# The product of gates and expert biases as one split product between the experts, with a dozen units in other slots

## The reference

```
x = x + attention(layernorm(x))                         # 16 heads of 64, rotary q and k, softmax
x = x + cross_attention(layernorm(x), context, mask)    # 16 heads of 64, + bout
x = x + experts(layernorm(x))

def experts(h):
    probs = softmax(h @ Wg)                             # 8 experts
    top_vals, top_idx = top_k(probs, 2)
    gates = top_vals / sum(top_vals)                    # two gates per token
    expert_out = h @ We + be                            # be: one bias row per expert
    return sum(gates * expert_out[top_idx])
```

## Time and profile before

| | |
|---|---|
| runs | 3580.51 us median of 3 (3579.56 to 3580.77) |
| profiled execution | span 3581.8 us from the first to the last instruction; no other time is given for it |
| PE busy | 3501.3 us (98%), 28992 products |
| PEld busy | 2949.8 us (82%) |
| DVE / ACT / POOL busy | 2358.7 (66%) / 2220.8 (62%) / 2121.2 us (59%) |
| DMA | 47.44 MB, 4.0% of the 16 engines' time for the main queue |
| chain of waits | PE 89%, DVE 5%, ACT 2%, issue 2%, POOL 2% |

### The profile page before, as it was taken

How to read it: one execution, slowest core, us unless ns; L and a number is a source line. 1 busy time by engine, 2 the same in 40 slices (tenths; PEclk the granted TensorE clock), 3 DMA queues, 4 the chain that set the end, 5 groups by cost and what they waited for, 6 DMA issues and landing times.

```text
span 3581.8 us, 80997 instructions
## 1 busy us (share of the span) xinstructions
PE 3501.3 (98%) x28992; PEld 2949.8 (82%) x28992; DVE 2358.7 (66%) x7401; ACT 2220.8 (62%) x6442; POOL 2121.2 (59%) x1928
## 2 busy tenths in 40 slices
PE   6899999999999999999999999999999999999998
PEld 5788888888888888888888888888888888888886
DVE  6666667666666666676666666666766667666665
ACT  5666666666666666666666666666666666666663
POOL 5555676555665556765556755566655567555662
PEclk8999999999999999999999999999999999999999
DMA  3100000000000000000000000000000000000000
GB/s 98 37 10 13 10 10 10 10 13 12 7 10 12 9 12 10 9 10 10 12 12 7 10 12 10 12 10 9 10 10 12 12 7 12 11 10 12 13 6 8
DMA packets 46796, 47.44 MB, mean 13 GB/s; under 512 B 8256, under 2 KB 43328, under 8 KB 46400
## 3 DMA queue, kind: packets, MB, share of 16 engines
q1 hardware_dynamic: 45696, 41.99, 4.0%
q10 hardware_dynamic: 704, 0.27, 0.0%
HBM read 33.86 MB, written 8.39 MB: 12 GB/s over the span
## 4 chain that ended last, share of the span: by engine, by line
PE 89%; DVE 5%; ACT 2%; issue 2%; POOL 2%; DMA 0%; ACTq 0%; POOLq 0%; DVEq 0%
PE unit_ps L536 19%; PE pT_ps L648 14%; PE oT_ps L665 14%; PE score_ps L632 11%; PE unit_ps L524 10%; PE wo_ps L690 10%; PE unit_ps L546 8%; DVE x L1021 1%; ACT probs L798 1%; POOL probs L1150 1%; DVE probs L936 1%; PE unit_ps L555 1%; DVE bn L863 1%; DVE x_in L1029 1%; ACT v_sb L744 1%
## 5 line engine op out<-in xcount | busy, mean ns | idle before, releaser
L1150 POOL TENSOR_TENSOR probs<-probs,inv_sum 128x512 f32<-128x512 f32 x1024 | 1062.1, 1041 | 956.4 <-DVE inv_sum L919 956.3
L787 ACT ACTIVATE pT<-pT_ps 128x512 f32<-128x512 f32 x1024 | 606.2, 594 | 136.1 <-PE pT_ps L648 135.5
L798 ACT ACTIVATE probs<-probs,neg_max 128x256 f32<-128x256 f32 x1024 | 508.9, 500 | 276.4 <-DVE probs L936 276.4
L648 PE MATMUL pT_ps<-ident,probs 128*128 128x128 f32 x4096 | 634.0, 279 | 13.2 <-POOL probs L1150 12.5
L648 PEld LDWEIGHTS pT_ps<-ident,probs 128*128 128x128 f32 x4096 | 451.8, 141 | 221.8 <-issue 204.0
L798 ACT ACTIVATE probs<-score_ps,neg_max 128x256 f32<-128x256 f32 x1024 | 476.6, 476 | 179.1 <-DVE neg_max L925 179.1
L665 PE MATMUL oT_ps<-pT,v_sb 128*64 128x256 f32 x4096 | 556.0, 392 | 4.4 <-ACT pT L787 4.0
L936 DVE TENSOR_SCALAR_CACHE_REDUCE probs<-score_ps,mask_add 128x256 f32<-128x256 f32 x1024 | 433.4, 480 | 104.8 <-PE score_ps L632 101.9
L536 PE MATMUL unit_ps<-xs_hi,w_lo 128*128 128x256 f32 x1536 | 460.1, 300 | 9.3 <-DVE swap L972 7.8
L536 PE MATMUL unit_ps<-xs_hi,w_hi 128*128 128x256 f32 x1536 | 436.6, 284 | 0.0
L536 PE MATMUL unit_ps<-xs_lo,w_hi 128*128 128x256 f32 x1536 | 436.1, 284 | 0.0
(11 more groups left out here) (121 smaller groups left out, 8573.0 us busy)
## 6 DMA issues: line engine op xcount, KB each, us to landing
x_in<-dram_x SPq DMA_DIRECT2D x32, 256.0 KB, 2.7
xn<-dram_ctx SPq DMA_DIRECT2D x32, 256.0 KB, 2.7
layer_out<-x SPq DMA_DIRECT2D x32, 256.0 KB, 2.2
swap<-dram_bout SPq DMA_DIRECT2D x32, 128.0 KB, 3.1
rope<-dram_be SPq DMA_DIRECT2D x32, 64.0 KB, 2.9
rope<-dram_we SPq DMA_DIRECT2D x5, 256.0 KB, 2.8
probs<-dram_sk SPq DMA_DIRECT2D x4, 256.0 KB, 5.1
x<-dram_cq SPq DMA_DIRECT2D x4, 256.0 KB, 3.2
```

Source lines behind the costliest of these rows:

```text
L648: last = nc.tensor.transpose(pT_ps[s % 2][:, k * T + t * P:k * T + (t + 1) * P], probs[:, hs % P_BUFS, t, k * P:(k + 1) * P], ident[:])
L787: nc.scalar.activation(flat(pT[:, s % 2, :, :]), pT_ps[s % 2][:], ACT.Copy).then_inc(pT_ready.sem, 1)
L798: last = nc.scalar.activation(dst, src, ACT.Exp, bias=neg_max[:, h % STATS, t:t + 1], scale=1.0 if h < H else -1.0, accum_out=row_sum[:, h ...
L1150: nc.gpsimd.tensor_tensor(weights, weights, inv.unsqueeze(2).to_broadcast([P, NT, T]), ALU.mult).then_inc(probs_ready.sem, 1)
```

## The change

Gates and biases are each taken as a high part (fp32r) and a low remainder, and the three products high x high, low x high and high x low are stacked along the 128 rows, so that one fp32r product gives the sum. Once, in the first pass, ACT and DVE split the biases and SP writes the parts to a DRAM tensor `be_parts` (rows of high, high, low and zeros, 32 each). In each pass SP loads them into the second half of `xs_hi` (slot 12), DVE copies the gates three times into 128 columns (slot 13, `gate_cols`), TensorE transposes those, DVE casts them to fp32r and subtracts for the low rows, in the first half of `xs_hi`. GT stands in slot 15 and BI in slot 16, between EX3 and EX4; the bias is added between those two experts' adds.

The table moves other units: V2 from slot 8 to 10, V3 from 10 to 13, EX3 from 14 to 15, K4 from 17 to 18, EX6 from 18 to 19, K5 from 19 to 22, Q5 from 21 to 20, V5 from 23 to 21, K6 from 22 to 26, Q6 from 24 to 23, K7 from 30 to 28, V6 from 27 to 29, V7 from 35 to 33. Some go from NOW to LATE or back, EX1 among them (now NOW). In slot 18 the order is EX5, the last self-attention projection, V4, K4, L2. The gate weights move to slot 7, the first layer norm (statistics and norm) one slot later. In slot 15 the projection now follows the units, in slot 27 it precedes them.

```diff
-    8: [("V", 2, 0, LATE), ("EX", 0, -1, LATE)],
-    9: [("EX", 1, -1, LATE)],
+    8: [("EX", 0, -1, LATE)],
+    9: [("EX", 1, -1, NOW)],
...
-    "gate weights": 8,
+    "gate weights": 7,
     "gate table": 8,
...
-        be_sb = rope[0:HD, 0, 0, 0:D]
-        gatesT, bout_sb = swap[0:HD, 0, 0:T], swap[:, 1, 0:D]
+        be_sb = rope[0:32, 0, 0, 0:D]
+        be_hi, be_lo = xf_hi[0:32, 0, 0:D], xf_lo[0:32, 0, 0:D]
+        gate_cols = xn[:, :, 0:P]
+        gatesT, be_rows = xs_hi[:, 0, 0:T], xs_hi[:, 1, 0:D]
...
+                    if s == AT["expert biases"] and exists(b, -1):
...
+                        sp.dma_start(be_rows.bitcast(F32), be_parts).then_inc(be_loaded.sem, 16)
...
-                        last = nc.tensor.transpose(ps[0:E, t * P:(t + 1) * P], gates[:, t, :], ident[:])
+                        last = nc.tensor.transpose(ps[:, t * P:(t + 1) * P], gate_cols[:, t, :], ident[:])
...
                         last = nc.tensor.matmul(ps[:, t * D:(t + 1) * D], gatesT[:, t * P:(t + 1) * P],
-                                                be_sb, start=True, stop=True)
+                                                be_rows, start=True, stop=True)
...
-                    nc.vector.tensor_copy(gatesT[0:E, :], ps[0:E, 0:T]).then_inc(gatesT_ready.sem, 1)
+                    nc.vector.tensor_copy(gatesT, ps[:, 0:T]).then_inc(gatesT_hi.sem, 1)
+                    dve.wait_ge(gatesT_hi.sem, gatesT_hi.at(b, off, 1))
+                    nc.vector.tensor_tensor(gatesT[32:64], ps[32:64, 0:T], gatesT[32:64].bitcast(F32),
+                                            ALU.subtract).then_inc(gatesT_ready.sem, 1)
...
+                        blocks = gate_cols.rearrange("p t (i e) -> p t i e", e=32)[:, :, 0:3, 0:E]
+                        nc.vector.tensor_copy(blocks, gates[:].unsqueeze(2).to_broadcast([P, NT, 3, E])) \
+                            .then_inc(gate_columns.sem, 1)
```

More of the change, by code:

```diff
@@ L98 @@
     1: [],
-    2: [("V", 0, 0, NOW), ("K", 2, 0, LATE)],
+    2: [("K", 2, 0, LATE), ("V", 0, 0, NOW)],
     3: [],
@@ L154 @@
     "norm 3": 5,
-    "gate weights": 8,
+    "gate weights": 7,
     "gate table": 8,
     "context": 11,
-    "mask": 13,
+    "mask": 14,
+    "gate columns": 13,
+    "expert biases": 12,
+    "expert biases split": 23,
     "statistics 2": [18, 0],
-    "norm 2": [18, 3],
+    "norm 2": [18, 1],
     "x to x1": 22,
-    "statistics 1": 24,
-    "norm 1": 25,
+    "statistics 1": 25,
+    "norm 1": 26,
     "last values": [17, 0],
@@ L166, with before_bias @@
     "residual 3": 3,
-    "projection first": [7, 15, 31],
+    "projection first": [7, 27, 31],
 }
-def bias_first(s):
-    return s % 2 == 0 and UNITS[s] and UNITS[s][0][0] == "BI"
+def before_bias():
+    added = sorted((s + late, 1 - late, n, kind) for s in UNITS for n, (kind, g, off, late) in enumerate(UNITS[s])
+                   if kind in ("EX", "BI"))
+    return [kind for _, _, _, kind in added].index("BI")
+BEFORE_BIAS = before_bias()
 def splits(b, s):
@@ L709, in body @@
                     for n, (kind, g, off, _) in enumerate(UNITS[s]):
-                        if exists(b, off) and not (n == 0 and bias_first(s)):
+                        if exists(b, off):
                             unit(b, s, n, kind, g, off)
@@ L836, in body @@
                         split_piece(j)
+                    if s == AT["expert biases split"] and isinstance(b, int) and b == 0:
+                        act.wait_ge(be_in, 16)
+                        nc.scalar.activation(be_hi, be_sb, ACT.Copy).then_inc(be_split, 1)
                 if isinstance(b, int) and b == -1:
@@ L1089, in body @@
                         gate_table(b, -1)
+                    if s == AT["gate columns"] and exists(b, -1):
+                        if exists(b, 0):
+                            dve.wait_ge(ctx_ready.sem, ctx_ready.at(b, 0, 1))
+                        else:
+                            dve.wait_ge(xf_turned.sem, xf_turned.at(b, -1, 1))
+                        dve.wait_ge(gate_step.sem, gate_step.at(b, -1, GATE_STEPS))
+                        blocks = gate_cols.rearrange("p t (i e) -> p t i e", e=32)[:, :, 0:3, 0:E]
+                        nc.vector.tensor_copy(blocks, gates[:].unsqueeze(2).to_broadcast([P, NT, 3, E])) \
+                            .then_inc(gate_columns.sem, 1)
+                    if s == AT["expert biases split"] and isinstance(b, int) and b == 0:
+                        dve.wait_ge(be_split, 1)
+                        nc.vector.tensor_tensor(be_lo, be_sb, be_hi.bitcast(F32), ALU.subtract).then_inc(be_split, 1)
                     if s == AT["mask"] and exists(b, 0):
```

90 lines of the change are left out of this document (58 added, 32 removed).

## The result

The changed kernel takes **3651.4 us** (median of 4 runs, 3650.0 to 3652.3), the kernel before 3580.4: ratio 1.020, 95% interval 1.019 to 1.021. Slower by 71 us: one round takes 111.57 us in place of 109.32, and 31 times 2.25 are 70. The prediction said 3602, range 3564 to 3614: the direction was right, the size a third of what came, and the time outside the range.

What follows compares the result with a forecast made beforehand. TensorE, busy 98% of the span, bounds the kernel. Per round -0.67 - 1.65 + 0.95 + 1.71 + 0.39 = +0.73 us, over 31 rounds +22.6, drain -0.8, added to 3580.5: 3602 us, range 3564 to 3614.

Steps and rivals of the forecast that it cites:

- New gap 2: Slots 8 to 11: gate weights ahead of DVE's reciprocal delay head 8; +1.71 us per round, bounds 0.5 to 1.9.
- shared-port rule: Gate table on DVE: a two-SBUF-input step or cast waits out a whole POOL instruction; steps of 1.1 us expected.
- Rival B: Slots 8 to 11: a table step gets between POOL's rope steps; gap about 1.0 us, 3580 us total; chance 0.13.
- New gap 1: Slot 18: L2 waits for the norm with only V4 and K4 between; +0.95 us per round, bounds 0.8 to 1.1.
- Q4's wait: Behind the late L2: Q4 waits 0.24 us for xs_lo, one of the small new gaps.
- The product: Product of gates and biases: two fp32r products over 128 rows, 0.24 us; -0.67 per round, bounds -0.5 to -0.8.
- L3 put at nothing: Slot 6: the prediction has no term for a new wait of L3.
- all of the 1.65 as gone: Whole round: all old gaps in TensorE's starts, 1.65 us per round, go; new ones are priced separately.
- POOL's stretch without a break: Slot 30 to slot 1: POOL has rope and probabilities throughout; head 0's probabilities end 0.46 us before its transposes.
- rival C: From slot 30 to slot 1 POOL becomes the bound; 1 us more per round, 3634 us; chance 0.07.
- I count 1.0 back: Slot 30 to slot 1: 1.44 us of TensorE products leave; 1.0 regained as K7's split no longer delays DVE and ACT.
- T0: Transposes of head 0's probabilities: a small new wait of 0.05 us per round.

Runs made afterwards that it cites:

- runs 1 to 3: Changed kernel with gate weights back in slot 8: 3630.6 us; changed kernel with V2, V3 back in slots 8, 10: 3605.8; kernel before with gate weights in slot 7: 3582.3.
- run 6: Changed kernel with V0 before K2 in slot 2, as before the change: 3631.8 us.
- run 9: Changed kernel with the product of gates and biases read as fp32, same 128 stacked rows and same place: 3675.1 us.
- Run 11: Kernel before with the split product alone, in its old slot 20: 3585.8 us, ratio 1.0013.
- run 5: Changed kernel with V6 in slot 30 instead of 29: 3663.6 us.
- 15: Changed kernel with V2, V3 back in slots 8, 10, V0 before K2, V6 in slot 30, Q0 LATE, V7 in slot 35: 3582.7 us.
- run 4: Changed kernel with Q0 before K7 in slot 28 instead of behind it: 3686.0 us.
- runs of 14: Changed kernel with V2, V3 back in slots 8, 10, V0 before K2, V6 in slot 30, Q0 LATE in slot 28: 3594.6 us.
- runs 7: Changed kernel with K5 in slot 18 before L2, and Q6, Q7, K6 moved forward to slots 22, 23, 25: 3821.1 us.
- run 10: Kernel before's table with the split product, gates turned in slot 15, product in slot 16, slot 20 without a unit: 3675.8 us.
- run 12: Kernel before with the split product in slot 20, V5 moved to slot 21 and Q6 to slot 23: 3726.4 us.

## Why the prediction was right in direction and wrong in size

**New gap 2: right.** 1.71 forecast, 1.71 measured (slot 12's scores at 13.24, forecast 13.25), by the mechanism named: the steps beside POOL of 1.29 and 1.25, and runs 1 to 3 show its two halves, order and cover. The shared-port rule of the Trainium skill ("SBUF — State Buffer", "Who interferes with whom") is borne out for a case that the trace of before did not show: a cast of 16 elements waits for a whole POOL step, 1.29 us for 0.17. Rival B, a race in which a table step gets ahead of POOL, did not happen in the changed kernel: the cast lost it in all 31 rounds. But it is real. In the 13 traces in which the cast meets that rope step it starts 0.016 to 0.029 us behind it in all 403 rounds, and runs through in 61 of them, 27 of these in run 6. In 8 of the 10 runs that have both kinds of round, the rounds in which it runs through are shorter by 0.24 to 0.28 us.

**New gap 1: right, too small.** 0.95 forecast, 1.11 measured, 0.15 behind L2 that I hadn't counted, and 0.15 of Q4's wait (0.24 forecast). The chain was right to the norm's end; left out were the 0.14 from there to L2's start, and that K4's low part, queued behind the norm, would hold up EX6. Bounds of 0.8 to 1.1 didn't hold what stands behind L2.

**The product: right, its saving set too high.** 0.67 forecast, 0.53 by rows; 0.64 is what run 9 gives for the same stacked product in fp32, in its new place. I had set 0.24 for a group that costs 0.32 behind transposes. Run 11 adds what I didn't ask: in its old place the saving is worth nothing, since slot 22 waits it away.

**L3 put at nothing was the step that failed.** The prediction takes "all of the 1.65 as gone" and prices new gaps one by one; for L3 in slot 6 there is no term, and it waits 0.81. The forecast followed POOL's stretch without a break to head 0's transposes and stopped there, but the stretch runs on to norm 3, and L3 waits for that. Runs 5, 6 and 15 take the 0.81 apart: 0.42 go with V0 ahead of K2 (V0's copy then leaves ACT early enough for the split of Q2, for which POOL waits), an order that the prediction doesn't mention; 0.36 go with V7 back in slot 35 (with V6 already in slot 30; V7 alone was not run). With V7 in slot 33 TensorE has 1.44 us less to do between slot 34 and slot 6, POOL as much as ever. V6 alone leaves L3's wait as it is (run 5).

The step inside rival C, "I count 1.0 back", was nearly right: it concerns T0, for which 0.05 were set and 0.21 came, and that goes with V6 in slot 30. Rival C had a chance of 0.07 and "1 us more per round". T0 and L3 together are 0.94 more than before's 0.08, so its size came true, but by luck: most of it comes from moves and a place that it doesn't name. That K7 is the unit whose place matters, the guess of run 4, was wrong too; the run shows it as L1's cover.

The sum: 0.73 forecast, 2.25 measured. Of the 1.52 between them L3 is 0.73 (0.81 less before's 0.08), L2 and the product behind it 0.31, T0 0.16, the bias product 0.14; the last 0.2 are gaps of about 0.1, L3's old 0.08 among them, which I had counted among those that go. That all 1.65 of old gaps go was nearly right: V4, K5 and slot 22 are gone.

**What stays open.** Slot 12's 0.17 and the waits of 0.1 behind the last projection were not tried. The runs of 14 lie between 3588.5 and 3597.2, and the profiled one, on which its round rests, is the lowest. A part of this can be the race: in the profiled execution the cast won it in 13 of 31 rounds (109.30 us against 109.57), so the same execution with every race lost would be 3.5 us longer, 3592 as an estimate. The rest is open. Why the clock falls in some rounds of runs 10 and 12 and not in others with the same waits is open too. A cover for the last 0.6 of L2's wait wasn't found: each unit tried was cover elsewhere.

## What to carry to other kernels

When an engine off the critical path works without a break over a stretch, follow it to the last thing that anyone waits for, not to the first: units that leave such a stretch are worth nothing and come back as waits. Before a short product is made shorter, look at what waits behind it; if it is a result that isn't ready, the product was cover. And a late result costs only what the critical engine has no work for: move the work before the order.

## What the runs showed of the hardware

- How small a DVE step is doesn't protect it from POOL. Beside a POOL tensor_tensor of 1.29 us a cast of 128x16 took 1.29 (0.17 alone), a tensor_tensor of 128x4 1.25 (0.16 at the least), a tensor_scalar of 128x8 1.34 (0.28). The reciprocal of 128x2 was not held up: 0.168 us at the most in 1024 of them.
- Hundredths of a microsecond go with who waits, without a sharp line. The cast with a recorded start 0.016 or 0.017 us behind POOL's ran through 20 times of 20, at 0.018 22 of 27, at 0.019 to 0.024 19 of 192, at 0.025 to 0.029 0 of 164. Where it ran through, POOL's step took 1.33 or 1.34 us in place of 1.29.
- A long wait of TensorE can cost more than itself. In runs 7, 10 and 12 the granted clock falls to 1.2 GHz, for 3.4 us as a rule, within 1.5 us of the end of waits of 3.8, 2.0 and 2.1 us, in all, 28 and 11 of 30 rounds. That costs 1.2 us (run 10) and 1.5 us (run 12) per fall; with the waits of 1.1 in the changed kernel it stayed at 2.4 GHz in all 30 rounds.
- The two fp32 products take no longer over 128 rows than over 64: 0.87 for the group in run 9, 0.95 in the earlier trace rows. The fp32r pair over 128 rows takes 0.32.
